# Neighbourhood sums of the later gated layers as two fp32r products, and a new order of steps

## The reference

```python
A = (adj != 0).astype(x.dtype)
h = x
for l in range(weight.shape[0]):                 # 5 layers
    m = jnp.einsum('bnd,de->bne', h, weight[l])
    agg = jnp.einsum('bij,bid->bjd', A, m)
    h = _gru_cell(agg, h, w_ih, w_hh, b_ih, b_hh)
```

## Time and profile before

| | |
|---|---|
| Time, median of 3 runs | 1730.95 us (1729.19 to 1732.3) |
| Time of the profiled execution | 1731.32 us, its span in the profile 1729.5 us |
| PE busy | 1622.2 us, 94% |
| PEld busy | 1328.9 us, 77% |
| DVE busy | 1365.5 us, 79% |
| ACT busy | 1313.4 us, 76% |
| POOL busy | 779.8 us, 45% |
| DMA | mean 24 GB/s |
| Chain that ended last | PE 79%, DVE 11%, ACT 7%, issue 2%, POOL 1% |

### The profile page before, as it was taken

How to read it: one execution, slowest core, us unless ns; L and a number is a source line. 1 busy time by engine, 2 the same in 40 slices (tenths; PEclk the granted TensorE clock), 3 DMA queues, 4 the chain that set the end, 5 groups by cost and what they waited for, 6 DMA issues and landing times.

```text
span 1729.5 us, 33712 instructions
## 1 busy us (share of the span) xinstructions
PE 1622.2 (94%) x12060; PEld 1328.9 (77%) x12060; DVE 1365.5 (79%) x3531; ACT 1313.4 (76%) x3122; POOL 779.8 (45%) x843
## 2 busy tenths in 40 slices
PE   4779999999999999999999999999999999999984
PEld 3567788787878878787887878788787878877763
DVE  5577897878789787878978787897978789787753
ACT  1467788787778878777887877788787778887763
POOL 2233454535445453544545354454535445453432
PEclk8799999999999999999999999999999999999997
DMA  3000100101010010101001010100101010000000
GB/s 89 21 24 20 30 13 26 29 13 30 25 29 14 26 29 13 30 25 30 14 26 29 14 29 26 29 13 26 28 14 29 26 29 14 25 14 13 13 7 12
DMA packets 84800, 40.92 MB, mean 24 GB/s; under 512 B 10629, under 2 KB 84634, under 8 KB 84634
## 3 DMA queue, kind: packets, MB, share of 16 engines
q1 hardware_dynamic: 84250, 38.64, 8.1%
q10 hardware_dynamic: 384, 0.13, 0.0%
HBM read 30.36 MB, written 8.39 MB: 22 GB/s over the span
## 4 chain that ended last, share of the span: by engine, by line
PE 79%; DVE 11%; ACT 7%; issue 2%; POOL 1%; POOLq 0%; DVEq 0%; ACTq 0%
PE RA L908 17%; PE RB L908 16%; PE Q L875 8%; PE RT L1084 8%; PE RT L875 4%; PE Q L1011 4%; ACT x L510 3%; PE M L875 3%; PE Q L1026 3%; PE M L943 2%; PE M L951 2%; PE Q L994 2%; DVE stats L638 2%; PE M L1054 2%; PE Q L998 2%
## 5 line engine op out<-in xcount | busy, mean ns | idle before, releaser
L493 POOL TENSOR_TENSOR h_lo<-hT,h_hi 128x512 fp32r<-128x512 f32 x160 | 210.5, 1316 | 547.7 <-ACT h_hi L587 518.8
L565 ACT ACTIVATE e_s<-Q,s_ng 128x128 f32<-128x128 f32 x1024 | 296.8, 401 | 19.2 <-DVE s_ng L746 17.4
L496 POOL TENSOR_TENSOR hd<-hT,nn 128x512 f32<-128x512 f32 x160 | 206.2, 1289 | 35.8 <-ACT nn L599 35.7
L593 ACT ACTIVATE tr<-RA,b_rz 128x512 f32<-128x512 f32 x160 | 114.6, 716 | 101.4 <-PE RA L908 101.4
L599 ACT ACTIVATE nn<-tr,wT 128x512 f32<-128x512 f32 x160 | 117.3, 733 | 96.5 <-DVE tr L797 96.5
L752 DVE TENSOR_TENSOR p_s<-Q,adjTe 128x512 f32<-128x512 f32 x256 | 172.0, 683 | 21.7 <-PE Q L875 21.6
L746 DVE TENSOR_REDUCE s_ng<-Q 128x4 f32<-128x512 f32 x256 | 167.8, 681 | 10.1 <-PE Q L1011 8.8
L793 DVE SCALAR_TENSOR_TENSOR un<-tr,un 128x512 f32<-128x512 f32 x160 | 109.7, 685 | 73.3 <-ACT un L596 73.0
L789 DVE TENSOR_TENSOR agg_lo<-RT,agg_hi 128x512 fp32r<-128x512 f32 x160 | 109.9, 687 | 72.0 <-ACT agg_hi L590 70.1
L875 PE MATMUL Q<-ident,e_s 128*128 128x128 f32 x1024 | 156.9, 277 | 9.5 <-ACT e_s L565 9.5
L875 PEld LDWEIGHTS Q<-ident,e_s 128*128 128x128 f32 x1024 | 125.4, 142 | 34.6 <-ACT e_s L565 14.0
(11 more groups left out here) (188 smaller groups left out, 4342.9 us busy)
## 6 DMA issues: line engine op xcount, KB each, us to landing
adjn<-in_adj_dram SPq DMA_DIRECT2D x32, 256.0 KB, 2.9
xin<-in_x_dram SPq DMA_DIRECT2D x32, 256.0 KB, 3.3
adjr<-in_adj_dram SPq DMA_DIRECT2D x32, 256.0 KB, 3.1
out_dram<-x SPq DMA_DIRECT2D x32, 256.0 KB, 2.4
adjc<-in_adj_dram SPq DMA_DIRECT2D x128, 4.0 KB, 1.9
xs<-in_x_dram SPq DMA_DIRECT2D x120, 16.0 KB, 1.7
W1s<-in_L_gnn_W_dram SPq DMA_DIRECT2D x1, 640.0 KB, 4.4
W2s<-in_L_gnn_W_dram SPq DMA_DIRECT2D x2, 320.0 KB, 5.4
```

The source lines that it names most:

```text
L493: pool.tensor_tensor(h_lo[g][:, :], hT[g][:, :], h_hi[g][:, :], ALU.subtract).then_inc(SG["h_lo"][g], 1)
L496: pool.tensor_tensor(hd[g][:, :], hT[g][:, :], nn[g][:, :], ALU.subtract).then_inc(SG["hd"][g], 1)
L565: ins = act.activation(e_s[:, j, c, :], Q[j][:, c * P:(c + 1) * P], ACT.Exp, bias=s_ng[:, j, c:c + 1])
L593: act.activation(tr[g][:, :], RA[:, :], ACT.Tanh, bias=b_rz[:, 0:1], scale=0.5).then_inc(SG["r_act"][g], 1)
```

## The change

1. For layers 1 to 4, ACT writes the transposed state to `tok_hi`, rounded to fp32r. The difference `tok_lo = RT - tok_hi`, also fp32r, is a new DVE instruction. Both are one buffer, shared by the two groups, in place of one `h_tok` per group.
2. The neighbourhood sum of these layers is, per graph, two fp32r products that accumulate, `tok_hi` and `tok_lo` each with `a_bin`, in place of one fp32 product. PE waits for both `h_tok` (the semaphore's name is kept) and `tok_lo` before the first. `a_bin` is now written as fp32r. Layer 0 still uses one fp32 product.
3. All eight strings of `MERGE` are new, so the three threads are interleaved differently on PE, DVE, ACT and POOL. Within a thread the order is the same.

```diff
@@ MERGE (8 strings, one shown)
-    tensor=("AARARRRBBRABARRBRRAARAARAARRBARARBRAARRBBABRRBRBRARRARARRRBARRARAABARABRBAARRRBRRRRAARRRARABAARAAABRRRRA",
+    tensor=("AARRARRRRBBBARBAARRARARRARAAARBARARARBRRRBRBRAARBRABARRRRBBRARBRABAABRRAAABRRRRAAARRRRRARABRAAARAARBARRR",
@@ buffers
-        a_bin = [sb(f"a_bin_{g}", [P, GB, P]) for g in range(NG)]
+        a_bin = [sb(f"a_bin_{g}", [P, GB, P], F32R) for g in range(NG)]
-        h_tok = [sb(f"h_tok_{g}", [P, GB, P]) for g in range(NG)]
+        tok_hi = sb("tok_hi", [P, GB, P], F32R)
+        tok_lo = sb("tok_lo", [P, GB, P], F32R)
@@ scalar, steps
                 elif kind == "turn" and k:
                     wait_g(act, "h_mm", g, it, k)
-                    act.activation(cols(h_tok[g]), RT[:, :], ACT.Copy).then_inc(SG["h_tok"][g], 1)
+                    act.activation(cols(tok_hi), RT[:, :], ACT.Copy).then_inc(SG["h_tok"][g], 1)
@@ vector, steps
+                elif kind == "turn" and k:
+                    wait_g(dve, "h_tok", g, it, k)
+                    dve.tensor_tensor(cols(tok_lo), RT[:, :], cols(tok_hi), ALU.subtract).then_inc(SG["tok_lo"][g], 1)
@@ tensor, steps
                         wait_g(pe, "h_tok", g, it, k)
-                    src = x3[g] if k == 0 else h_tok[g]
+                        wait_g(pe, "tok_lo", g, it, k)
                     for q in range(GB):
-                        ins = pe.matmul(RT[:, q * P:(q + 1) * P], src[:, q, :], a_bin[g][:, q, :], start=True, stop=True)
+                        o = RT[:, q * P:(q + 1) * P]
+                        if k == 0:
+                            ins = pe.matmul(o, x3[g][:, q, :], a_bin[g][:, q, :].bitcast(F32), start=True, stop=True)
+                        else:
+                            pe.matmul(o, tok_hi[:, q, :], a_bin[g][:, q, :], start=True, stop=False)
+                            ins = pe.matmul(o, tok_lo[:, q, :], a_bin[g][:, q, :], start=False, stop=True)
                     ins.then_inc(SG["agg_mm"][g], 1)
```

More of the change, by code:

```diff
@@ L43 @@
 PER_GRU = dict(
-    a_bin=1, nm3=1, x3=1, x3t_mm=1, h_first=1, h_mm=LAYERS - 1, h_tok=LAYERS - 1,
+    a_bin=1, nm3=1, x3=1, x3t_mm=1, h_first=1, h_mm=LAYERS - 1, h_tok=LAYERS - 1, tok_lo=LAYERS - 1,
     agg_mm=LAYERS, agg_t=LAYERS, r_mm=LAYERS, hn_mm=LAYERS, in_mm=LAYERS, zg_mm=LAYERS,
@@ L51 @@
 MERGE = dict(
-    tensor=("AARARRRBBRABARRBRRAARAARAARRBARARBRAARRBBABRRBRBRARRARARRRBARRARAABARABRBAARRRBRRRRAARRRARABAARAAABRRRRA",
[L53 to L59, removed]
+    tensor=("AARRARRRRBBBARBAARRARARRARAAARBARARARBRRRBRBRAARBRABARRRRBBRARBRABAABRRAAABRRRRAAARRRRRARABRAAARAARBARRR",
+            "RRAABRRARRARARARRRRBRAARAAARBARARRABABRARARRBRARAABRARARABRABRRAARARBARBRARRRRRRRRRAARAAAARARRRRA"),
+    vector=("AARRRABBRRABRAAAARARRBRARARAAAARRRAABRARRRRBRBBBRBRRBRAAAARBRRRABRBBRRRABABAARRARARRRARARRRRARAARARBARRA",
+            "RRARARARRAARRRARBRAARAARARARAABRARRABARARBRBRRABARBAAARAAARRAARRRBBRRRAARARBRRRRRRRRRRAAAAARRRBAR"),
+    scalar=("AARRBABRRRBRARAAARBRARARRAARRBARABBRBRARRRRAARARBARRBARRARARRRBAABRABRRAABRRABAAARBRRRARARRABRRAAARBRRRA",
+            "RRAARRAARBRRARRARRBRARARAAARRRRAAAAABBRRABRRARBAARARARBRBAAARRRBARRRRARARARABRRRARRARAARRAARRARRB"),
+    gpsimd=("RRABRARABRRRRRARRARABABAAARRRAAARARRRRABBRBRRBRBRRARRRARRRRARRRRRRBBARBAAAARBRABBRBAARAAAAAAARAARRBABARR",
+            "RRARAAARARRARBRRRRRRBRBRRRRARAABBBAARRAAAAARARRRRABRARRBRARRRARRRBAAAAARARRAARRBRARRARAAAABARRRRA"),
 )
```

## The result

The changed kernel takes 1770.1 us (median of 4 runs, 1768.5 to 1770.6), the kernel before 1731.6 in the same job (1729.2 to 1733.1): a ratio of 1.0224, 95% interval 1.0212 to 1.0236, 38.5 us slower. Forecast were 1742 and a range up to 1765. The profiled execution has a span of 1768.4 us where the one before had 1729.5.

The account below looks back on a forecast made before the run. PE was taken to bound the steady iteration (busy 98.7 of 100.8 us). Products 0, drain 6.7, steady turns 4.2 and between the halves 0 made 10.9 on 1731.3, so a median of 1742 us; range 1715 to 1765.

Parts of the forecast that it names:

- The products: `agg` on PE, layers 1 to 4: weight loads set the time, so two fp32r products cost the same; change 0.
- (b): Rival: columns bound `agg`, so PE gains by the products; -56 + 11, 1686 us; chance 0.04.
- (d): Rival: narrow fp32r products on PE are as dear as wide ones; +120, 1860 us; chance 0.03.
- The drain: Near the end nothing hides `tok_lo` between `turn` and `agg`: nine turns at 0.74, +6.7 us.
- The steady turns: Steady iterations, `turn` to `agg`: cover slightly short for `tok_lo`, 0.3 x 14 = +4.2 us (0 to 35).
- the plain shortfall of the tightest place: Steady `turn` to `agg`: 0.2 us per iteration taken, out of 0 to 1.9, as with free engines.
- four tight places: Four of eight turns per iteration have about 2.0 to 2.2 us cover; 0.3 later each if DVE is busy.
- rival (c): DVE's queue becomes the bound; half of 5.5 us shows in the period, 2.75 x 14 + 7 = 45, 1776 us; chance 0.15.
- Between the halves: Between an iteration's halves: moved `o_ts` and DVE's reordered steps change nothing; 0 (down to -3 us).
- So it is given back: 0: Between the halves: `o_ts` some 0.2 us earlier on ACT, lost again at the wait for `on_ts`; 0.
- the 0 for `x`: Between the halves: DVE's four `x`, now behind `nm_0` and `hd`, count 0, since ACT is occupied until then.
- Rival (a): New lists close PE's gaps between the halves: 1710 to 1724 us, deciding from 0.75 us per iteration; chance 0.22.

Follow-up runs that it names:

- e4: Kernel before's order with the changed kernel's eight fp32r products, but no `tok_lo` (second product reads `tok_hi`, low part left out): ratio 1.0003.
- e2: Kernel before (one fp32 product, no `tok_lo`) with the new `MERGE` strings alone: 18.8 us slower than the kernel before.
- e11: Changed kernel with `tok_lo` and its wait left out in the last iteration alone: 1766.7 us, 1.0207.
- e3: Changed kernel, new order, without `tok_lo` and its wait; second product reads `tok_hi`, still eight products: 1752.0 us.
- e7: Changed kernel with DVE's instruction kept but fed from `tok_hi`, `agg` not waiting for it, both products reading `tok_hi`: 1756.4 us, 1.0142.
- e12: Kernel before with one move alone, ACT's `o_ts` copy ahead of `nn` in both halves: 1731.6 us, 1.0003.
- e9: Kernel before's sums in the new order, with three PE steps meant to be put back to their old places: 1751.3 us, 1.0126.
- e8: Kernel before's order with one fp32r product per graph, no `tok_lo`, low part left out: 1708.9 us, 0.9872.
- f6: Changed kernel, new order, with one fp32r product per graph, no `tok_lo`, low part left out: 1717.3 us, 0.9918.
- f5: Changed kernel with four small DVE steps put behind `tok_lo` instead of ahead of it: 1778.1 us, 1.0269.

## Why the prediction was wrong

**The products: right.** "Change: 0 x 128 = 0": PE's work is 95.10 us per iteration with either kind, and e4 equals the kernel before within 0.1%. Rivals (b) and (d) are out. The rule of the Trainium skill in "TensorE: Matmul & The Clock Gate", LDWEIGHTS, 107 ns for 128 columns, agrees with the 0.11 between the records. By the four passes for true fp32 that the Trainium skill states in "FP8 and Floating Point Precision", TensorE Precision Notes, two single-pass products could have been cheaper; at this width e4 shows no gain.

**The drain: right.** 9 x 0.74 = 6.7 forecast; the tail grew 9.2 us over that of e2, 5.7 of them by the last iteration's eight turns (e11). The rest lies at turns of the iteration before it, which the tail holds too and which I had counted as steady.

**The steady turns: mechanism right, size wrong.** Forecast 4.2 us for fourteen iterations, measured 10.0 for 11.7 of them (e2 to after), 0.86 each, so 12.0 for fourteen. I had set the need at 2.08 to 2.22 with "the plain shortfall of the tightest place", that is, DVE free when ACT's copy ends. At the worst place it was 0.91 late, behind work that the new string itself puts ahead of `tok_lo`; its `agg` starts 3.02 after `turn`, where in e3 it does so after 2.36, which was cover enough for my need. At the second place it is 2.48 instead of 2.10. My own mean, 0.3 at each of four tight places, would have given 1.2 per iteration, nearer to the 0.91 by which the table's sum grows; I took its least part. My rival (c), that DVE's load shows in the period, is real where DVE alone carries the load, but small: 0.42 us per iteration (e3 to e7), not 2.75.

**Between the halves, and the order as a whole: the step that failed.** "So it is given back: 0" holds for `o_ts` (e12 shows where), and the stall on DVE only changed its victim, as forecast. In groups of DVE over seven iterations, before and after:

```profile
L656 DVE TENSOR_SCALAR x<-xin,mv,rs 128x128 f32<-128x128 f32 x57 | 22.6, 458 | 0.0
...
L652 DVE SCALAR_TENSOR_TENSOR nm<-mv,rs 128x4 f32<-128x4 f32 x28 | 11.8, 422 | 1.0
```

```profile
L653 DVE SCALAR_TENSOR_TENSOR nm<-mv,rs 128x4 f32<-128x4 f32 x28 | 19.3, 691 | 2.2 <-POOL rs L448 0.2
...
L657 DVE TENSOR_SCALAR x<-xin,mv,rs 128x128 f32<-128x128 f32 x56 | 15.6, 343 | 0.0
```

`nm` went from 422 to 691 ns and `x` from 458 to 343, 34.4 and 34.9 us together. Between the halves one `nm` takes 1.23 us, from 930.17, with POOL's `hd` running from 930.10 to 931.37, where it took 0.15 before. That is what "SBUF — State Buffer", Who interferes with whom, in the Trainium skill would have `nm` suffer. But the 0 for `x` was false as a place: PE now waits 0.41 for it, and has exactly that back at `xT`. What I never priced was the rest of the new strings. I read them at the turns and between the halves and let everything else stand as it was. The order alone costs 11.6 us in 11.7 iterations, 1.0 each, at `hT`, `o_ns` and `begin`, and 6.2 up to step 31, which holds 2.3 iterations of its own (some 4 us of it an execution can differ by itself), 18.8 us by the medians. That is two thirds of the 28 us by which I missed. Rival (a) had the right waits, `o_ts` and `xT`, and they shrank by 0.70 us per iteration, near its 0.75; the new order lost 1.7 net at the other places.

The sum, measured in the span: products 0, order 17.8 (1729.5 to 1747.3), steady turns 11.8 (10.0, and the 1.8 ahead of step 31, since the first turns of the two executions are 0.1 apart), tail 9.2, in all 38.8 of the 38.9. The split into order and `tok_lo` holds in the new order only: in the old one `tok_lo` alone costs 99.6.

**What stays open.** Why this order is 18.8 us slower with the sums of before is located, by the table, and for the 0.48 per iteration at the end turn traced to four transposes that left its cover, but no run gets it back. The test that would settle it, `M<-ident,f_t` behind `agg` in e2, was not made; e9 moved one step that exists, and two halves and four engines taken alone made it worse or made other losses. Why a shorter `agg` is worth 34.7 us in it and 22.1 in the old one is open too; the idle time that PE gets in its place stands in the main at `hT`, 0.9 more per iteration in e8 than in e4 and 0.7 more in f6 than in e3.

## What to carry to other kernels

An instruction that is put into a dependence of a list-scheduled kernel costs its latency plus what stands ahead of it in its engine's list at that moment; read that list from the order, don't assume the engine free. A change that brings a new order for all engines is two changes: price the order by its own, at every wait of the bounding engine and not only at the places that the new instruction touches, and measure the old work in the new order first. A wait removed by moving one step is no gain until the next instruction of the same engine's list is earlier too (f5, e9, e12). And before a moved step is taken for a test, see in the trace that its instructions moved: two of the three steps of e9 had none on PE.

## What the runs showed of the hardware

For four graphs eight fp32r products of 128 columns take PE the time of four fp32 products, 8 x 0.112 us; in the whole kernel the ratio is 1.0003 [0.9993, 1.0012] (e4). Near the end the hand-over from DVE to PE took 0.12 us (`tok_lo`, 1662.27 to 1662.39) where that from ACT took 0.05. And two executions whose programs are alike up to step 31 reach it 3.6 us apart (383.3 and 386.9), as much as the differences that some of these runs were to tell.
